# Node rows written ahead: the edge stage stores h, x + b2 and skip as one row a node, and the node stage loads that row

## The reference, cut to what matters

```python
h = jnp.maximum(_layernorm(x, axis=-1), 0.0)          # h, of every node
# L0(h): z = layer_norm(h)
skip = z @ Wskip.T + bskip
out  = segment softmax over the edges into a node of (q[dst] . (k[src]+e)), times (v[src]+e)
beta = sigmoid(concatenate([out, skip, out - skip]) @ Wbeta.T)
x_l  = h + beta * skip + (1.0 - beta) * out
y    = x_l + relu(layer_norm2(x_l) @ W1.T + b1) @ W2.T + b2
x1   = x + y                                          # x + L0(h)
h2   = jnp.maximum(_layernorm(x1, axis=-1), 0.0)
result = x1 + L1(h2)                                  # second convolution
```

## Time and profile before

| | |
|---|---|
| median of 3 runs | 4261.69 us (4200.47 to 4282.03) |
| profiled execution | 4272.86 us, span 4271.1 us |
| busy in the span | PE 2449.4, PEld 1993.8, DVE 2146.2, ACT 1716.7, POOL 2380.6 us |
| granted clock of TensorE, mean | 0.774 of 2.4 GHz |
| DMA | 479.31 MB, mean 112 GB/s |
| gathers of the edge stage (L239) | 2 x 392, 949 and 948 ns each |

### The profile page before, as it was taken

How to read it: one execution, slowest core, us unless ns; L and a number is a source line. 1 busy time by engine, 2 the same in 40 slices (tenths; PEclk the granted TensorE clock), 3 DMA queues, 4 the chain that set the end, 5 groups by cost and what they waited for, 6 DMA issues and landing times. The chain is left out here.

```text
span 4271.1 us, 56176 instructions
## 1 busy us (share of the span) xinstructions
PE 2449.4 (57%) x13730; PEld 1993.8 (47%) x13730; DVE 2146.2 (50%) x8636; ACT 1716.7 (40%) x4322; POOL 2380.6 (56%) x2380
## 2 busy tenths in 40 slices
PE   0015666677777676757887887888533333343344
PEld 0004666666666666644555555555432232233334
DVE  8982443443444443466666666666311111466567
ACT  7962222232222222236666666667311111333233
POOL 7765444454454444426555555544466665677675
PEclk9998888788888888878888888888755555555555
DMA  6542322232333223243433434433355555345565
GB/s 209 191 149 65 104 89 87 85 108 86 97 101 105 86 89 106 88 112 118 127 113 115 121 113 120 125 103 102 85 118 113 109 120 107 109 123 121 119 134 118
DMA packets 275117, 479.31 MB, mean 112 GB/s; under 512 B 58939, under 2 KB 167880, under 8 KB 274968
## 3 DMA queue, kind: packets, MB, share of 16 engines
q1 hardware_dynamic: 211214, 343.45, 25.4%
q0 software_dynamic: 63424, 133.57, 15.5%
q10 hardware_dynamic: 378, 1.26, 0.1%
HBM read 293.29 MB, written 186.18 MB: 112 GB/s over the span
## 5 line engine op out<-in xcount | busy, mean ns | idle before, releaser
L239 POOL DMA_INDIRECT zs<-z_table,src_col x392 | 372.1, 949 | 667.7 <-PE p_tr L822 486.7
L1380 PE MATMUL p_f<-z_t,w_t 128*128 128x512 f32 x784 | 448.3, 736 | 176.7 <-ACT z_t L1427 119.7
L1768 POOL DMA_INDIRECT aggc<-rows,node_row x392 | 444.0, 1133 | 181.6 <-issue 117.6
L1608 POOL DMA_INDIRECT h2s<-h_table,src_col x392 | 372.0, 949 | 202.0 <-issue 111.1
L1336 POOL DMA_INDIRECT agg<-rows,at_n x392 | 394.9, 1007 | 113.7 <-issue 112.8
L239 POOL DMA_INDIRECT zd<-z_table,dst_col x392 | 371.6, 948 | 125.1 <-issue 121.4
L1689 PE MATMUL p_sum<-h2s,same 128*128 128x129 f32 x784 | 191.7, 420 | 391.1 <-issue 184.9
L1390 PE MATMUL p_f<-w_t,act 128*128 128x128 f32 x3136 | 376.5, 278 | 0.5 <-issue 0.5
L1380 PEld LDWEIGHTS p_f<-z_t,w_t 128*128 128x128 f32 x784 | 182.5, 240 | 415.1 <-issue 378.4
L808 PE MATMUL p_v<-wsk_t,zn_t 128*128 128x129 f32 x784 | 161.9, 340 | 369.5 <-issue 367.3
L1390 PEld LDWEIGHTS p_f<-w_t,act 128*128 128x128 f32 x3136 | 357.5, 192 | 22.2 <-issue 22.2
(11 more groups left out here) (323 smaller groups left out, 6727.8 us busy)
## 6 DMA issues: line engine op xcount, KB each, us to landing
rows<-rows_sb SPq DMA_DIRECT2D x49, 576.0 KB
skip_table<-skip_sb SPq DMA_DIRECT2D x49, 516.0 KB
skipb<-skip_table SPq DMA_DIRECT2D x49, 516.0 KB
h_table<-h2b SPq DMA_DIRECT2D x49, 516.0 KB
rows<-rows_sb SPq DMA_DIRECT2D x49, 516.0 KB
xa<-in_x_dram SPq DMA_DIRECT2D x49, 512.0 KB
z_table<-za SPq DMA_DIRECT2D x49, 512.0 KB
zn<-z_table SPq DMA_DIRECT2D x49, 512.0 KB
```

What stands on the lines that cost most here:

```text
L239: pool.indirect_dma_start(out=to[:, slot, k], out_offset=None, in_=z_table, in_offset=bass.IndirectOffsetOnAxis(ap=col[:, g * G + k:g * G ...
L1380: t_.matmul(p_f1[c][:, :], w1_t[:, c * P:(c + 1) * P], z2_t[:, q].rearrange("p a b -> p (a b)"), start=True, stop=True).then_inc(S["f1_don ...
L1608: pool.indirect_dma_start(out=h2s[:, slot, k], out_offset=None, in_=h2_table, in_offset=bass.IndirectOffsetOnAxis(ap=src_col[:, g * G + k: ...
L1768: pool.indirect_dma_start(out=agg[:, slot, k], out_offset=None, in_=rows1, in_offset=bass.IndirectOffsetOnAxis(ap=node_row[:, g, k:k + 1], ...
```

## The change

The edge stage gets the node's whole row ready for the node stage: skip and its gate part (129 numbers), h (128), x + b2 (128), 385 numbers in `node_sb`, stored as one row of `node_table` (1540 KB a group). For this SP loads x once more (`xe`, 512 KB a group), ACT makes h there (`keep_h`, two tiles in each of the four units, before `copy_v`), DVE adds b2 (`add_b2`, after `count`) and copies the norms. The node stage loads that row in one transfer, and has no `h_of`, no copy of the norms and no bias product; its down product starts its banks itself. The splitting of b2 into bf16 parts goes.

```diff
-    skip_table = dram("skip_table", [N, D + 1])
+    node_table = dram("node_table", [N, NODE])
...
                             sp.dma_start(zn[:, slot], rows).then_inc(zn_in[slot], 16)
+                            at_least(sp, h_kept, 4 * (g - 1))
+                            at_least(sp, xb_kept, 4 * (g - 1))
+                            hold(sp, held)
+                            rows = x[bass.ds(first_row(g), GR), :].rearrange("(p t) d -> p t d", t=G)
+                            sp.dma_start(xe[:, slot], rows).then_inc(xe_in[slot], 16)
...
-                            rows = skip_table[bass.ds(first_row(g), GR), :].rearrange("(p t) d -> p t d", t=G)
-                            sp.dma_start(rows, skip_sb[:, slot]).then_inc(skip_out[slot], 16)
+                            sp.wait_ge(xb_kept, 4 * g + 4)
+                            hold(sp, held)
+                            rows = node_table[bass.ds(first_row(g), GR), :].rearrange("(p t) d -> p t d", t=G)
+                            sp.dma_start(rows, node_sb[:, slot]).then_inc(skip_out[slot], 16)
...
                         act.wait_ge(node_skipped, 4 * g + n + 1)
-                        if n == 0:
+                        a.activation(node_sb[:, slot, 2 * n:2 * n + 2, 0:D + 1], p_skip.rearrange("p (t c) -> p t c", t=2), ACT.Copy).then_inc(skip_kept, 1)
+
+                    def keep_h(g, slot, use, u):
+                        if u == 0:
+                            act.wait_ge(xe_in[slot], 16 * (use + 1))
+                            act.wait_ge(norm_set, g + 1)
                             at_least(act, skip_out[slot], 16 * use)
-                        a.activation(skip_sb[:, slot, 2 * n:2 * n + 2], p_skip.rearrange("p (t c) -> p t c", t=2), ACT.Copy).then_inc(skip_kept, 1)
+                        for k in (2 * u, 2 * u + 1):
+                            last = a.activation(node_sb[:, slot, k, D + 1:2 * D + 1], xe[:, slot, k], ACT.Relu,
+                                                bias=norm_e[:, slot, 1, k:k + 1], scale=norm_e[:, slot, 0, k:k + 1])
+                        last.then_inc(h_kept, 1)
 
                     def copy_sums(g, slot, use, u):
                         act.wait_ge(summed, 4 * g + u + 1)
...
                             copy_nodes(*new, 0)
                             copy_z(*new, 1)
+                            keep_h(*new, 0)
                             copy_v(*new, 0)
...
+                                keep_h(*new, u + 1)
                                 copy_v(*new, u + 1)
                             if old:
...
 
+                    def add_b2(g, slot, use, u):
+                        if u == 0:
+                            dve.wait_ge(xe_in[slot], 16 * (use + 1))
+                            at_least(dve, skip_out[slot], 16 * use)
+                        v.tensor_tensor(node_sb[:, slot, 2 * u:2 * u + 2, 2 * D + 1:NODE], xe[:, slot, 2 * u:2 * u + 2],
+                                        b2_row[:].unsqueeze(1).broadcast_to([P, 2, D]), ALU.add).then_inc(xb_kept, 1)
+
                     def message(g, slot, use, u):
...
+                            at_least(dve, h_kept, 4 * (g - 1))
+                            v.tensor_copy(norm_e[:, slot], stats[:, bass.ds(g, 1)].rearrange("p a b c -> p (a b) c")).then_inc(norm_set, 1)
...
                     v.memset(wea1[:], 0.0).then_inc(zeroed, 1)
                     v.memset(wea[:], 0.0).then_inc(zeroed, 1)
                     chain = Chain(dve, e0_step)
-                    chain.mark(v.memset(ones3[:], 1.0))
...
-                            rows = x[bass.ds(first_row(g), GR), :].rearrange("(p t) d -> p t d", t=G)
-                            sp.dma_start(x_sb[:, ring], rows).then_inc(x_in[ring], 16)
-                            rows = skip_table[bass.ds(first_row(g), GR), :].rearrange("(p t) d -> p t d", t=G)
-                            sp.dma_start(skip_sb[:, ring], rows).then_inc(skip_in[ring], 16)
+                            rows = node_table[bass.ds(first_row(g), GR), :].rearrange("(p t) d -> p t d", t=G)
+                            sp.dma_start(node_sb[:, ring], rows).then_inc(node_in[ring], 16)
...
                         for k in range(4):
                             for c in range(4):
-                                last = t_.matmul(p_f2[q][:, k * D:(k + 1) * D], act1[:, q, c, k * P:(k + 1) * P], w2_t[:, c], start=False, stop=(k == 3 and c == 3))
+                                last = t_.matmul(p_f2[q][:, k * D:(k + 1) * D], act1[:, q, c, k * P:(k + 1) * P], w2_t[:, c], start=(c == 0), stop=(c == 3))
                         last.then_inc(S["f2_done"], 1)
 
...
                     a = nc.scalar
-
-                    def h_of(g, slot, use, ring, lap, tiles):
-                        if 0 in tiles:
-                            act.wait_ge(x_in[ring], 16 * (lap + 1))
-                            act.wait_ge(S["tab_ready"], g + 1)
-                            at_least(act, S["base_ready"], g - WAYS + 1)
-                        for k in tiles:
-                            last = a.activation(h_sb[:, ring, k], x_sb[:, ring, k], ACT.Relu, bias=norm[:, ring, 1, k:k + 1], scale=norm[:, ring, 0, k:k + 1])
-                        if G - 1 in tiles:
-                            last.then_inc(S["h_ready"], 1)
 
                     def z2_of(g, slot, ring, q):
...
                             h2_of(last[0], last[1], last[2], range(6, G))
-                        if fetch:
...
-                            dve.wait_ge(S["h_ready"], g + 1)
                             v.tensor_tensor(base[:], base[:], h_sb[:, ring], ALU.add).then_inc(S["base_ready"], 1)
                             dve.wait_ge(S["base_ready"], g + 1)
...
-                                last_ = v.scalar_tensor_tensor(x_l[:, slot, k], skip_sb[:, ring, k, 0:D], gate[:, k:k + 1], base[:, k], ALU.mult, ALU.add)
+                                last_ = v.scalar_tensor_tensor(x_l[:, slot, k], skip_sb[:, ring, k], gate[:, k:k + 1], base[:, k], ALU.mult, ALU.add)
                             last_.then_inc(S["xl_ready"], 1)
...
-                            v.tensor_tensor(x_xl[:, ring], x_l[:, slot], x_sb[:, ring], ALU.add).then_inc(S["xxl_ready"], 1)
+                            v.tensor_tensor(x_xl[:, ring], x_l[:, slot], xb_sb[:, ring], ALU.add).then_inc(S["xxl_ready"], 1)
                             dve.wait_ge(S["norm2_ready"], g + 1)
```

More of the change, by code:

```diff
@@ L46 @@
 ROW0 = MSG + H2
+NODE = 3 * D + 1
 DV = D + H
@@ L200, in build @@
         bq_row = sb("bq_row", [P, D])
-        b2_row = sb("b2_row", [3, D])
+        b2_row = sb("b2_row", [P, D])
         bkv = sb("bkv", [P, 2, D])
@@ L666, in build @@
             zn, zn_t = t("zn", [P, 2, G, D]), t("zn_t", [P, 2, 2, P])
-            skip_sb = t("skip_sb", [P, 2, G, D + 1])
+            node_sb = t("node_sb", [P, 2, G, NODE])
+            xe, norm_e = t("xe", [P, 2, G, D]), t("norm_e", [P, 2, 2, G])
+            xe_in = [s(f"e0_xe_in{a}") for a in range(2)]
+            norm_set, h_kept, xb_kept = s("norm_set"), s("h_kept"), s("xb_kept")
             p_alpha, p_back, p_ea = p_small[0:G * H, 0:P], p_small[:, P:P + 2 * G * H], p_small[:, 256:256 + P]
@@ L679, in build @@
             wea_wa = t("wea_wa", [META, D])
-            part1, part2, part3 = (t(f"bias_part{n}", [3, D], BF16) for n in range(3))
-            rest, mixed3 = t("bias_rest", [3, D]), t("mixed3", [3, D])
             zeroed, wea1_done, wea1_set, wea_done, e0_step = s("zeroed"), s("wea1_done"), s("wea1_set"), s("wea_done"), s("e0_step")
@@ L1142, in half @@
                                 count(*new, u)
+                                add_b2(*new, u)
                     v.memset(wea1[:], 0.0).then_inc(zeroed, 1)
@@ L1145, in _ @@
                     chain = Chain(dve, e0_step)
-                    chain.mark(v.memset(ones3[:], 1.0))
                     chain.mark(v.memset(metag[:], 0.0))
-                    for row, n, parts, times in ((b2_row[:], D, b2_parts, 4),):
-                        chain.step(v.tensor_copy(part1[:, 0:n], row))
-                        chain.step(v.tensor_tensor(rest[:, 0:n], row, part1[:, 0:n], ALU.subtract))
-                        chain.step(v.tensor_copy(part2[:, 0:n], rest[:, 0:n]))
-                        chain.step(v.tensor_tensor(rest[:, 0:n], rest[:, 0:n], part2[:, 0:n], ALU.subtract))
-                        chain.step(v.tensor_copy(part3[:, 0:n], rest[:, 0:n]))
-                        chain.step(v.tensor_scalar(mixed3[:, 0:n], part1[:, 0:n], ident[0:3, 0:1], None, ALU.mult))
-                        chain.step(v.scalar_tensor_tensor(mixed3[:, 0:n], part2[:, 0:n], ident[0:3, 1:2], mixed3[:, 0:n], ALU.mult, ALU.add))
-                        chain.step(v.scalar_tensor_tensor(mixed3[:, 0:n], part3[:, 0:n], ident[0:3, 2:3], mixed3[:, 0:n], ALU.mult, ALU.add))
-                        for j in range(times):
-                            chain.mark(v.tensor_copy(parts[:, j * n:(j + 1) * n], mixed3[:, 0:n]))
-                        chain.wait()
```

(9 more changed lines are left out.)

18 lines of the change are left out of this document (6 added, 12 removed).

## The result

| | before | after |
|---|---|---|
| median, 5 runs each | 4261.69 us (4200.47 to 4288.75) | 3927.54 us (3909.35 to 4061.98) |
| profiled execution: time, span | 4272.86, 4271.1 us | 4009.91, 4008.2 us |
| up to the node stage (ACT's first `z_t` copy there) | 1938.2 | 1884.5 |
| node stage, first to last such copy | 1075.8 | 856.0 |
| from there to the end | 1257.1 | 1267.7 |

The ratio is 0.925 (95% 0.919 to 0.931): 7.5% faster, where I forecast 1.7%.

The account below looks back on a forecast made before the run. No engine was full; results released late while POOL issues gathers were taken to hold the edge and node stages. 4272.9 - 18 + 14 - 75 = 4194, rounded to 4190 us (own range 4145 to 4230, overall 4115 to 4335).

Parts of the forecast that it names:

- (2): Node stage: eight activations for h, 3.17 us a group, go from ACT; 0 us, since PE would be late next.
- (1): Node stage: two bias products a group go, 0.62 us of PE; counted in 28 groups, -18 us.
- (9): Edge stage: ACT's first pair of h waits for the node store; delay of 1.3 us mostly hidden, +14 us.
- (10): Edge stage: PE later against POOL's second burst, so more bursts pause and 65% of periods are short; -75 us.
- my own sign of being wrong: Edge stage: the value copy starts later than 10 us behind the store, which would mean C.
- C: Rival, edge stage: the node store lands late and nothing hides it; 101 us more, 4370 us, slower; chance 0.17.
- (3) to (8): Node stage: norms copy gone, one wider load; edge stage: ACT's activations, DVE's additions, b2 splitting gone, x load; each 0.
- The rule on ports: Node stage: if PE and ACT never waiting at ports covered release of results, 31 us saved, sum 13 us lower.

Follow-up runs that it names:

- e1: Changed kernel with eight activations of 128x128 put back on ACT in the node stage and DVE waiting for them; late chip, 3914.06 us.
- e2: Changed kernel with the two bias products a group (of zeros) put back on PE in the node stage; late chip, 4089.39 us.
- e3: Changed kernel with both ACT's eight activations and PE's bias products put back in the node stage; late chip, 4143.28 us.
- e6: Kernel before without the two bias products a group, b2 missing in its output; prompt chip, 3211.39 us against 3257.84.
- e17: Kernel before with one wait more, a pause in POOL's second burst of gathers in the edge stage; prompt chip, 3255.29 us (0.998).
- e9: Changed kernel unchanged, run on a prompt chip beside the kernel before; 3548.94 us (1.088).
- e4: Kernel before with one wait more: POOL's node-stage gathers start after PE's two down products of the step before; late chip, 3987.85 us (0.934).
- e11: Changed kernel with two tables: skip apart from h and x + b2, each with own store and semaphore, h made later; prompt chip, 3209.98 us (0.986).
- the first and the fifth set: Two of six sets of follow-up runs, each on one chip together with the kernel before, which took 4271.90 and 4295.78 us there.
- e12: e11 with POOL's node-stage gathers also waiting for PE's down products of the step before; prompt chip, 3212.67 us (0.985).
- e14: Repeat of e12, two tables and gathers held, on a prompt chip; 3215.60 us (0.990).
- e13: Repeat of e11, two tables, on a prompt chip; 3204.93 us (0.984).

## Why the prediction was wrong, step by step

The traces that I had were of a late chip, and so was the result. There:

- **(2), ACT's eight activations: 0.** Right, e1. That "what would be late next is PE itself" was right too.
- **(1), the bias product: -18, at most -31.** This is the step that failed: the product was sized at 18 us (28 x 0.62 is 17.4), and the runs give it 162 us (the changed kernel to e2) and 229 us (e1 to e3; e2 and e3 scatter over 203 and 146 us), on a prompt chip 46 us (e6); the node stage of the trace is 220 us shorter. It failed twice. In size: the product costs PE 0.93 us a group, not 0.62: in e17's node stage the way from the end of the up product to the next transposes is 8.07 us with it (2007.94 to 2016.01), in e9's 7.14 without (2006.09 to 2013.23); I took the distance of two starts and left out that the two down products behind it take 7.44 us with it (2008.25 to 2012.02, 2012.34 to 2016.01) and 7.14 without. In mechanism, and more weighty: I counted a late release as a cost that a group has or hasn't, 28 groups against 17. It is one that the group before hands on. A microsecond less of PE let 27 to 45 groups leave that mode, for 5.6 us each and more. I had the short mode before me in the earlier trace rows, took it for "no gathers", and read POOL's start as given by DVE and POOL, so as swallowing any gain, though DVE's start hangs on PE. The single executions and e3's 24 short groups say that chance, or something untested, has a part in how many groups change over.
  PE's timeline in the node stage, e17 (with the product), then e9 (without):

```profile
2007.94 0.39 PE L1391 MATMUL p_f<-b_parts,ones 3*128 3x512 bf16 x1
2008.25 3.84 PE L1394 MATMUL p_f<-w_t,act 128*128 128x128 f32 x32
2012.02 0.38 PE L1391 MATMUL p_f<-b_parts,ones 3*128 3x512 bf16 x1
2012.34 3.84 PE L1394 MATMUL p_f<-w_t,act 128*128 128x128 f32 x32
2016.01 1.04 PE L1377 MATMUL p_t<-ident,z 128*128 128x128 f32 x8
```

```profile
2006.09 7.31 PE L1400 MATMUL p_f<-w_t,act 128*128 128x128 f32 x64
2013.23 1.04 PE L1384 MATMUL p_t<-ident,z 128*128 128x128 f32 x8
```

- **(9) and (10), the edge stage: +14 and -75, sum -61.** Measured -54, and partly by luck. h begins 7.6 to 8.2 us behind the store's issue in the steady groups (8.0 said). ACT's wait before it is 5.2 us in the mean, not "some 3"; the earlier trace rows had ACT free 2.5 us behind the issue, which gives 5.5. The value copy stands at 8.4 to 11.8, median 8.9 (8.9 said). In 17 of 45 groups it is over 10 us, my own sign of being wrong, but not for C's reason: the store has landed and h is done, and the copy starts within 1 us of the end of POOL's first burst. The late release is paid again there, which (9) didn't have. Of 43 second bursts 37 are split (65% was said), but a split one no longer makes a period of 27.9: 24 of them have 28.9 us in the mean, 13 have 30.9. More splits, each worth less, gave nearly the sum. Over all groups 31.1 became 30.1 us. The size is not well settled: the node stage begins at 1883.5 to 1899.6 us in e1, e2 and e3, which have the changed edge stage, and at 1938.2 before but 1908.5 in e4, which has the old one; that makes 9 to 55 us.
- **(3) to (8): 0.** Nothing speaks against it; e11, on a prompt chip, does all this work at the old edge period. The later stages took 10.6 us more in the one trace.
- **The rivals.** Of C one half, that nothing hides the landing, is what happens on prompt chips, at 7.4 us a group and not 2.2; its other half, a late landing, is not: there too h begins 8.1 us behind the issue. I had written that the delay "is hidden", since "that is when they start today, for the late release": that cover was the late release itself. Without it the step (9) is +340 and not +14. I named the cover and didn't price its absence, as I took the late release for a trait of the machine.
- **The rule on ports.** The Trainium skill, "SBUF — State Buffer", section "Who interferes with whom", says that PE and ACT never wait at their ports. On late chips a result is late while POOL issues, on prompt ones it isn't, with the same gathers, so the ports alone don't hold it; what does, no run here shows.

## What to carry to other kernels

Where the idle time in front of an instruction follows another engine's rhythm, ask whether a group's delay makes the next group's: then look for the edge between two modes, tie the start of the disturbing burst to the end of the disturbed work (e4: one wait, 284 us on a late chip; on prompt ones the same wait costs 3 and 11 us, e12 against e11 and e14 against e13), and don't price a microsecond at a microsecond. A step that is free because something else is late anyway must be priced with that cover gone: here it was the whole sign. Ask for a store's landing where it has long landed, with a buffer and a semaphore of its own.

## What of the hardware was not expected

- The same program takes 3256 to 3260 us on three chips, and 4262, 4272 and 4296 us where the first traces, the first and the fifth set ran, with nearly equal gathers (0.95 and 0.96 us, one each 1.25). The difference is in how late engines learn of results while POOL issues: in the first trace's edge stage the first value copy of a group stands 7.4 us behind the store's issue in the mean of 45, on prompt chips 3.4.
- On prompt chips scatter is small (3247 to 3273 us over 46 runs of the kernel before); on late ones 4200 to 4324.
- PE's granted clock is higher where it isn't held up: 0.84 of 2.4 GHz in the edge stage before, 0.99 on a prompt chip.
